# Where the layer norm's bias is added in a four-layer Mamba scan kernel: on GpSimd, or on ScalarE and TensorE

## The reference, cut to what matters

```python
for i in range(N_LAYERS):                        # 4
    y = _mamba(x, in_proj_w[i], conv_w[i], ..., out_proj_w[i])
    x = _layer_norm(y + x, ln_w[i], ln_b[i])     # (x - mu) * rsqrt(var + eps) * w + b

# inside _mamba: a projection in, a convolution over 4 tokens, silu, three small projections,
# a softplus, and for each of 512 channels and 16 states the scan
#   h = h * exp(delta * A) + delta * u * B;   y = sum over states of h * C
# then y * silu(z), and a projection out.
```

## Time and profile before

| | |
|---|---|
| median of 3 runs | 7999.23 us (7994.17 to 8001.62) |
| the profiled execution | 7997.37 us |
| its span in the profile | 7995.6 us |
| VectorE busy | 7676.5 us, 96% of the span |
| GpSimd busy | 7305.0 us, 91% |
| TensorE busy | 6415.5 us, 80% |
| ScalarE busy | 5655.9 us, 71% |
| mean granted TensorE clock | 0.91 of full |

### The profile page before, as it was taken

How to read it: one execution, slowest core, us unless ns; L and a number is a source line. 1 busy time by engine, 2 the same in 40 slices (tenths; PEclk the granted TensorE clock), 3 DMA queues, 4 the chain that set the end, 5 groups by cost and what they waited for, 6 DMA issues and landing times. The chain is left out here.

```text
span 7995.6 us, 76775 instructions
## 1 busy us (share of the span) xinstructions
PE 6415.5 (80%) x21028; PEld 2498.3 (31%) x21028; DVE 7676.5 (96%) x7155; ACT 5655.9 (71%) x9845; POOL 7305.0 (91%) x3828
## 2 busy tenths in 40 slices
PE   6888787888888887888887887878888888875888
PEld 2223232232323322233322332323332233322555
DVE  8999999999999999999999999999999999995777
ACT  5777777777777777777777777777777777763444
POOL 3999999999999999999999999999999999995555
PEclk7999999998899999899899999899899998887999
DMA  6444544555445445454444544455444454441110
GB/s 186 121 118 117 121 120 117 120 127 124 120 116 126 114 116 121 117 138 117 118 119 118 125 118 115 119 130 127 118 119 119 116 124 117 119 121 48 39 39 26
DMA packets 568087, 909.35 MB, mean 114 GB/s; under 512 B 60417, under 2 KB 202241, under 8 KB 566401
## 3 DMA queue, kind: packets, MB, share of 16 engines
q1 hardware_dynamic: 567680, 904.74, 46.2%
HBM read 715.55 MB, written 188.94 MB: 113 GB/s over the span
## 5 line engine op out<-in xcount | busy, mean ns | idle before, releaser
L926 POOL TENSOR_TENSOR hc<-h,crep 128x1024 f32<-128x1024 f32 x2048 | 4782.3, 2365 | 225.0 <-PE acc L483 181.7
L1081 DVE TENSOR_TENSOR_SCAN h<-dA,carry,bu 128x512 f32<-128x512 f32 x3072 | 3676.5, 1258 | 25.8 <-POOL hc L926 23.5
L636 ACT ACTIVATE dA<-drep,cur 128x512 f32<-128x512 f32 x4096 | 2620.9, 713 | 0.3 <-issue 0.3
L1066 DVE TENSOR_TENSOR bu<-durep,B_all 128x1024 f32<-128x1024 f32 x2048 | 2389.6, 1212 | 21.4 <-PE B_all L464 12.6
L464 PE MATMUL B_all<-dtc,spread_b 128*128 128x512 f32 x2048 | 1273.4, 707 | 1078.6 <-DVE bu L1066 1074.3
L483 PE MATMUL acc<-hc,gather 128*32 128x512 f32 x8192 | 1320.7, 698 | 105.8 <-ACT sums L755 86.2
L645 ACT COPY carry<-h 128x4 f32<-128x4 f32 x1023 | 199.8, 195 | 1396.2 <-DVE h L1081 1394.0
L1081 DVE TENSOR_TENSOR_SCAN h<-dA,bu 128x512 f32<-128x512 f32 x1024 | 1164.5, 1199 | 19.0 <-POOL hc L926 12.0
L507 PE MATMUL work<-xT,inw 128*128 128x512 f32 x2048 | 995.6, 625 | 120.4 <-ACT x_res L745 106.3
L517 PE MATMUL work<-xs,taps 128*128 128x512 f32 x2048 | 945.6, 604 | 3.4 <-ACT xs L673 3.4
L464 PEld LDWEIGHTS B_all<-dtc,spread_b 128*128 128x128 f32 x2048 | 367.1, 206 | 1765.3 <-DVE bu L1066 1643.2
(11 more groups left out here) (180 smaller groups left out, 7126.7 us busy)
## 6 DMA issues: line engine op xcount, KB each, us to landing
drep<-delta_dram SPq DMA_DIRECT2D x1024, 256.0 KB, 5.6
durep<-du_dram SPq DMA_DIRECT2D x1024, 256.0 KB, 8.3
crep<-c_dram SPq DMA_DIRECT2D x1024, 64.0 KB, 2.6
delta_dram<-za SPq DMA_DIRECT2D x64, 768.0 KB, 3.5
du_dram<-relu SPq DMA_DIRECT2D x64, 768.0 KB, 3.8
x_res<-xbuf SPq DMA_DIRECT2D x64, 512.0 KB, 4.5
xbuf<-x_res SPq DMA_DIRECT2D x64, 512.0 KB, 2.9
xc<-xbuf SPq DMA_DIRECT2D x63, 512.0 KB, 4.4
```

The costliest lines, as they stand in the source:

```text
L636: act.activation(dA[:, 4 * (s % 2) + k, :], drep[q % 2][:, k, :], ACT.Exp, scale=cur[:, p_, 4 * s + k:4 * s + k + 1]).then_inc(da_ready, 1)
L926: pool.tensor_tensor(hc[:, pair, :], h[:, pair, :], crep[:, j:j + 1, :].to_broadcast([P, 2, T]), ALU.mult).then_inc(hc_ready, 1)
L1066: dve.tensor_tensor(bu[:, 2 * k:2 * k + 2, :], durep[q % 2][:, 2 * k:2 * k + 2, :], B_all[:].unsqueeze(1).to_broadcast([P, 2, T]), ALU.mul ...
L1081: dve.tensor_tensor_scan(h[:, r, :], dA[:, r, :], bu[:, k, :], start, ALU.mult, ALU.add).then_inc(scanned, 1)
```

## The change

From the second layer on, the bias of the layer before is no longer in the stored x: `xbuf` and `x_res` hold the norm without its bias. It comes in where x is used. `copy_xT`, which copies the transposed x from PSUM to SBUF with channels on the partitions, becomes an activation with a bias of one number for each partition. `project_out` gets one more matmul for each 128 tokens, identity times lnb, where lnb holds the bias of the layer before in all partitions. GpSimd's second `affine` step remains only for the 16 chunks of the last layer, in the same place (`add_last_bias`), from a tile of its own. In the others, `x_ready` comes from the weight's multiplication at s = 0. Two small loads join the constants at the start.

```diff
@@ SyncE
-                sp.dma_start(lnb[:], w["lnb"][layer].partition_broadcast(P)).then_inc(post_w, 16)
+                sp.dma_start(lnb[:], w["lnb_before"][layer].partition_broadcast(P)).then_inc(post_w, 16)
...
+                             (w["lnbT"], lnbT[:]), (w["lnb_last"].partition_broadcast(P), lnb_last[:])):
@@ TensorE, project_out
                     pe.matmul(half, ident[:], x_res[:, t, :], start=True, stop=False)
+                    if m >= CH:
+                        pe.matmul(half, ident[:], lnb[:], start=False, stop=False)
@@ TensorE and VectorE
-            pe.wait_ge(consts, 80)
+            pe.wait_ge(consts, 112)
@@ ScalarE, copy_xT
-                    act.copy(xT[:, d, :], W[d][:]).then_inc(w_read[d], 1)
+                    if n < CH:
+                        act.copy(xT[:, d, :], W[d][:]).then_inc(w_read[d], 1)
+                    else:
+                        act.activation(xT[:, d, :], W[d][:], ACT.Identity,
+                                       bias=lnbT[:, n // CH, d:d + 1]).then_inc(w_read[d], 1)
@@ GpSimd
-            def affine(m, k):
...
+            def weigh(m):
+                pool.wait_ge(normed, m + 1)
+                pool.wait_ge(post_w, 48 * (m // CH) + 48)
+                pool.tensor_tensor(x_res[:], x_res[:], lnw[:].unsqueeze(1).to_broadcast([P, NT, D]),
+                                   ALU.mult).then_inc(weighted if m >= TOT - CH else x_ready, 1)
+
+            def add_last_bias(m):
+                if m >= TOT - CH:
+                    pool.wait_ge(weighted, m - (TOT - CH) + 1)
+                    pool.tensor_tensor(x_res[:], x_res[:], lnb_last[:].unsqueeze(1).to_broadcast([P, NT, D]),
                                        ALU.add).then_inc(x_ready, 1)
...
                         if s == 0:
-                            affine(g - 2, 0)
+                            weigh(g - 2)
                         if s == 2:
-                            affine(g - 2, 1)
+                            add_last_bias(g - 2)
```

More of the change, by code:

```diff
@@ L90, in mamba_layers @@
         outw = sb("outw", [P, DB, D])
-        lnw, lnb = sb("lnw", [P, D]), sb("lnb", [P, D])
+        lnw, lnb, lnb_last = sb("lnw", [P, D]), sb("lnb", [P, D]), sb("lnb_last", [P, D])
+        lnbT = sb("lnbT", [P, NL, KD])
         par = sb("par", [P, NL, NA])
@@ L364, in _ @@
             load_raw(0)
-            for src, dst in ((w["par"], par[:]), (w["biases"], biases[:]), (w["spread_b"], spread_b[:]), (w["gather"], gather[:]), (w["ident"], ident[:])):
+            for src, dst in ((w["par"], par[:]), (w["biases"], biases[:]), (w["spread_b"], spread_b[:]), (w["gather"], gather[:]), (w["ident"], ident[:]),
+                             (w["lnbT"], lnbT[:]), (w["lnb_last"].partition_broadcast(P), lnb_last[:])):
                 sp.dma_start(dst, src).then_inc(consts, 16)
@@ L1043, in _ @@
             gate(TOT - 1, 1, DB - 1)
-            for k in range(2):
-                affine(TOT - 2, k)
+            weigh(TOT - 2)
+            add_last_bias(TOT - 2)
             mean(TOT - 1)
@@ L1048, in _ @@
             newton_step(TOT - 1)
-            for k in range(2):
-                affine(TOT - 1, k)
+            weigh(TOT - 1)
+            add_last_bias(TOT - 1)
         @block.vector
@@ L1084, in work_out_a @@
                 a_log = par[:]
-                dve.wait_ge(consts, 80)
+                dve.wait_ge(consts, 112)
                 dve.tensor_scalar(a_k, a_log, 1.4426950408889634, ROUND, ALU.mult, ALU.add).then_inc(a_step, 1)
@@ L1752, in mamba_arrays @@
             spread[R + 4 * j + k, j, k] = 1
+    ln_b = w("ln_b")
+    before = np.concatenate([np.zeros_like(ln_b[:1]), ln_b[:-1]])
     return {
@@ L1760, in mamba_arrays @@
         "lnw": w("ln_w"),
-        "lnb": w("ln_b"),
+        "lnb_before": before,
+        "lnb_last": ln_b[-1],
+        "lnbT": np.ascontiguousarray(before.reshape(NL, -1, P).transpose(2, 0, 1)),
         "par": np.ascontiguousarray(by_state),
```

## The result

The changed kernel takes 8038.31 us (median of 5 runs, 8036.57 to 8039.99), the kernel before beside it 8001.62 us (7994.17 to 8004.74): a ratio of 1.0046, with a 95% interval of 1.0035 to 1.0057. It is slower by 36.7 us, where the forecast said 8032 us and 34 us.

A forecast was written before the change was run, and what follows sets the result against it. VectorE's own work (96% busy) was taken as the bound, with TensorE setting GpSimd's steps 6 and 7. Terms 39.6 + 2 - 10.1 + 2.5 + 1 - 1 = +34 us on 7997.4 us gave 8032 us, range 7985 to 8052.

The forecast's parts named there:

- What the change removes: Bias off GpSimd in turns 2 to 49: 2.35 us a turn becomes longer waiting at step 6, gain 0.
- What it adds at step 6: Two matmuls in project_out's second half delay GpSimd's step 7 and stall VectorE: 46 x 0.86 = +39.6 us.
- The spill at step 5: In a few turns TensorE's 1.76 us wait is used up, so the first half's 0.86 us shows: +2 us (0 to 5).
- The layer starts: Turns 17, 33, 49: x_ready 16 us earlier lets store and loads go earlier: -10.1 us.
- copy_xT: Its bias makes the copy 667 against 578 ns, at step 10, where ScalarE has time to spare: 0.
- The tail: After the last turn nothing covers project_out and TensorE starts cold; four matmuls at 0.43 to 0.85 us: +2.5 us.
- The start: Two more constants delay the queue's later loads at the start by 2 x 0.47 us: +1 us (0 to 2).
- The stalls at step 4: Two isolated stalls at step 4 may go: -1 us.
- The rule on the clock: Idling halves TensorE's rate, so added matmuls might take 0.86 us each; the forecast kept 0.43, from the profile's rows.
- The faster rival: GpSimd's load is what counts, so its removed 2.35 us carries through the wait: 7957 us, chance 0.15.
- the hidden one: TensorE's extra work is hidden by slack before the sums of step 5: 7991 us, no change, chance 0.15.
- The one at half clock: The added matmuls run at half clock, 46 x 1.72 = 79 us, with more spill at step 5: about 8075 us, chance 0.04.

The follow-up runs named there:

- experiment 4: The changed kernel with four additions to an unread tile on GpSimd at step 2, where the bias stood: 8034.09 us, ratio 1.0044 to the kernel before.
- experiment 3: The changed kernel with the bias matmuls in project_out's second half alone (step 6): 8029.55 us, ratio 1.0039 to the kernel before.
- Experiment 8: The changed kernel with the norm's weight on GpSimd at step 1 instead of step 0: 7985.45 us, ratio 0.9979 to the kernel before.
- Experiment 2: The changed kernel with the bias matmuls in project_out's first half alone (step 5): 7994.37 us, ratio 0.9996 to the kernel before.
- experiment 1: The changed kernel without project_out's bias matmuls, so the residual lacks the bias: 7989.06 us, ratio 0.9988 to the kernel before.
- 5: The kernel before, GpSimd's bias in place, plus project_out's four added matmuls on a tile of zeros from the second layer on: 8048.69 us, ratio 1.0058.
- experiment 11: The kernel before with the weight at step 1 and, at layer starts, outw loaded ahead of store_x on its own semaphore: 7967.6 us, ratio 0.9965.
- experiment 6: The changed kernel with the identity matmuls (x_res and bias) of project_out's second half issued at the end of step 5: 8009.02 us, ratio 1.0008; output wrong.
- experiment 7: The changed kernel with project_out's second-half identity matmuls at step 5, x_res as one 512-column matmul starting the whole bank: 8004.65 us, ratio 1.0011.
- 9: The changed kernel with the weight at step 1 and project_out's second-half identity matmuls at step 5, with two starts: 7992.87 us, ratio 0.9985.
- 10: The kernel before with only the norm's weight on GpSimd moved from step 0 to step 1: 7978.79 us, ratio 0.9979.

## Why the prediction was right

- **What the change removes** (2.35 us of GpSimd in 48 turns, gain 0). Right: experiment 4 puts it back, and the time stays within its interval.
- **What it adds at step 6** (46 x 0.86 us = 39.6 us). Right in place, size and way: experiment 3 measures 40.5 us, which holds a part of the tail; the wait at step 7 grew by 0.87 us, the second half of project_out takes 5.45 us in every turn from 17 to 62, and the stalls came at step 3 and in first chunks before step 14. The count is one too high: turn 63 has no silu_xc before step 1 and no stall at step 3, so turn 62's 0.86 us isn't paid. Experiment 8 shows both ways: moving the weight removes the one at step 3, and the one before step 14 stays.
- **The spill at step 5** (+2 us, up to 5). The size is too small, though within its bounds. Experiment 2 gives 5.3 us with its share of the tail. The cover of 1.76 us was read in one turn. In the kernel before, the same wait is over 1.7 us in 10 of 63 turns, between 0.6 and 1.7 in 44, and nothing in 9. The clock has a part in this, which the forecast took as 1.00 from one turn as well. In five turns of the trace after (31, 39, 46, 53, 55) GpSimd's step 6 starts over 1 us late, and each of them costs about 1 us. They are the five in which the granted clock is 0.50 all the way from B_all and the sums ahead of project_out's first half into it. In turn 31 TensorE stood idle for 2.91 us before them, and the granted clock from 3628 to 3633 us is 0.50:

```profile
3632.55 1.22 PE L545 MATMUL work<-x_res,ident 128*128 128x256 f32 x2
3633.56 1.06 PE L547 MATMUL work<-lnb,ident 128*128 128x256 f32 x2
```

  The first new matmul takes 0.85 us from its start to the next one's (3634.41 - 3633.56), not 0.43. It does so, or nearly (0.78 to 0.85 us), in 11 of the 47 turns; the second new matmul of that half and both of the second half take 0.43 us in all of them.
- **The layer starts** (-10.1 us). Right in size: experiments 1 and 5 give 9 us for all that is left of the change, the start's loss included. The mechanism is shown by the row of turn 17 and by experiment 11.
- **copy_xT** (0). It takes 672 ns instead of 578, as its neighbour did, and turn by turn nothing in VectorE's waits answers to it; it wasn't tried alone.
- **The tail** (+2.5 us). The span after the last scan grew by 2.8 us, but that it fits is luck. The last chunk's project_out takes 11.92 us before and 11.99 after: with the new matmuls TensorE comes to full clock at an earlier one of the others. Over all traces it takes 10.5 to 11.9 us without the four matmuls and 12.0 to 13.0 with them, so some 1 us. The rest of the 2.8 us lies in the feed-forward part, whose length varies by some 4 us from trace to trace and is as long in experiment 1 (670.2 us from its first transpose on, 669.4 after the change, 666.3 before), without the matmuls.
- **The start** (+1 us). Mis-sized: the first scan came 2.1 us later. I counted two issues on the queue. TensorE's first work now waits for a new constant:

```profile
10.39 1.97 PE L499 MATMUL work<-ident,h 128*128 128x128 f32 x8 [10.39 <-DMA lnb_last<-in_lnb_last]
```

  That is only 0.11 us later than it began before (10.28). What makes up the rest wasn't tried. It is no accident of one trace: within experiments 5 to 11 too the kernels with the two constants begin their scans 2 to 3 us later than those of the same group without. Over all traces they begin at 135.8 to 137.7 us, the others at 132.7 to 135.6.
- **The stalls at step 4** (-1 us). They didn't go: two turns had one (0.58 us each, turns 22 and 29), and after the change three have a smaller one (0.25 to 0.4 us).
- **The rule on the clock.** The Trainium skill ("TensorE: Matmul & The Clock Gate", Part 1) says that idling brings the half rate and sustained work the full one. By it the added matmuls could have cost double after a wait. The trace agrees, and shows both: PEclk 1.00 and 0.43 us in the second half of project_out, where it matters most; 0.50 and 0.85 us at step 5 of turn 31; and at the tail, after 13.86 us of idling, 0.50 and a first new pair of 1.06 us, where the later ones took 0.59 at 1.00.

The terms that were off (spill too small, start too small, tail too large, stalls at step 4 that stayed) are of a few us each and partly cancel; that the sum came within 3 us is in part luck. What carries it, 39 us against 10 us, was right by itself.

The faster rival fell by experiments 1 and 4, the hidden one by experiment 3. The one at half clock is true of some turns at step 5, where it is part of the spill, and false at step 6, where it would have doubled the loss. What failed were my expectations of 6, 9, 10 and 11: 6 took the cover of one turn for all, 9 and 10 took a cover or a stall from usual turns and forgot that the first chunks have another next bound, and 11 took the layer starts' stalls from the kernel before.

## What to carry to other kernels

Where one engine waits for another at a known place, work taken off it ahead of that wait is worth nothing, and work put on the other engine just before the place it waits for can cost its full time, however idle that engine is on average. In this kernel that was 0 for 2.35 us of GpSimd and 0.86 us for 0.86 us of TensorE. A cover read in one turn is one sample: look at it in all of them before a sum rests on it. Follow an engine's list from its last forced wait to the place where the bounding engine waits for it: what lies between is the path. Here it was cheaper to move the weight behind the product that VectorE waits for, one line, than to take the bias away.

## What was not expected of the hardware

Two matmuls that each start one half of a PSUM bank, the second while the first half is still being summed, gave a wrong sum (experiment 6). One start over all 512 columns and the same additions after it did not (experiment 7). The times are alike, 1.0008 and 1.0011 of the kernel before. With each half summed to its end before the next is started, as in the kernel before, the sums are right.
